# Beginning stage two with the token group that still lies in SBUF: order 2, 0, 1, 3

## The reference, cut to what matters

```
x = x + tanh(g_xattn) * (fake_quant(layernorm(x)) @ fake_quant(ctx))      # stage one
h = layernorm(x)                                                          # stage two
base = h @ base_W.T                                                       # 2048 x 2048
w = softmax top-2 of 8 experts, from h @ router_W.T
inc = ((h @ lora_A) * w) @ lora_B                                         # rank 16, 8 experts
x = x + tanh(g_ffn) * (base + 2.0 * inc)
```

## Time and profile before

| | us |
|---|---|
| median of three runs | 1121.61 |
| profiled execution, its time | 1117.15 |
| profiled execution, its span | 1115.4 |
| TensorE busy | 1027.0 (92%) |
| mean granted TensorE clock | 0.98 |

### The profile page before, as it was taken

The page is one execution under the profiler, slowest core; times in us unless marked ns, Lnnn a source line. Parts: engine busy times, 40 slices in busy tenths (PEclk is TensorE's granted clock), DMA queues, the critical chain, the costliest instruction groups (busy, mean ns, idle before and its releaser), DMA issues.

```text
span 1115.4 us, 12717 instructions
## 1 busy us (share of the span) xinstructions
PE 1027.0 (92%) x4827; PEld 762.8 (68%) x4848; DVE 768.4 (69%) x1046; ACT 448.1 (40%) x480; POOL 345.4 (31%) x181
## 2 busy tenths in 40 slices
PE   0588996999889999999999999899999989999998
PEld 0233442444378788788888878688887868888887
DVE  7696568882758754446778768986876898666554
ACT  5555155420043222223444445454444445434432
POOL 3685567769613433633100004400000350000000
PEclk9998998999979999999999999999999999999999
DMA  8998798887967787943585785568578456668754
GB/s 331 324 320 253 256 290 260 321 236 273 337 250 293 270 315 267 366 161 104 169 327 181 266 283 166 196 209 335 189 252 286 159 198 221 210 197 274 266 194 179
DMA packets 119052, 278.45 MB, mean 250 GB/s; under 512 B 40656, under 2 KB 48848, under 8 KB 110800
## 3 DMA queue, kind: packets, MB, share of 16 engines
q1 hardware_dynamic: 68048, 235.69, 59.1%
q10 hardware_dynamic: 50944, 41.95, 12.9%
HBM read 218.89 MB, written 50.33 MB: 241 GB/s over the span
## 4 chain that ended last, share of the span: by engine, by line
PE 68%; DVE 10%; DMA 7%; issue 4%; ACT 4%; POOL 4%; ACTq 2%; SPq 1%; POOLq 0%; DVEq 0%
PE acc L1380 16%; PE acc L1382 16%; PE acc L1381 16%; PE acc L1358 11%; DVE w_lo L1144 3%; DMA w_sums_scratch<-t_job 2%; DMA w_stage<-w_sums_scratch 2%; PE aT_psum L1450 2%; DMA out<-c_acc 2%; ACTq L808 2%; PE aT_psum L1428 1%; PE aT_psum L1429 1%; ACT ctx_u L795 1%; DVE A_lo L1245 1%; POOL ctx_quant L667 1%
## 5 line engine op out<-in xcount | busy, mean ns | idle before, releaser
L1144 DVE TENSOR_TENSOR w_lo<-w_stage,w_hi 128x1024 fp32r<-128x1024 f32 x200 | 268.0, 1351 | 170.1 <-ACT w_hi L853 169.2
L853 ACT ACTIVATE w_hi<-w_stage 128x1024 fp32r<-128x1024 f32 x200 | 209.6, 1058 | 355.5 <-PE acc L1382 266.0
L710 POOL TENSOR_TENSOR S_sum<-hT_A,hT_A 128x1024 f32<-128x1024 f32 x18 | 52.7, 2956 | 354.0 <-ACT hT_A L876 314.0
L1380 PE MATMUL acc<-w_hi,S_hi 128*128 128x512 f32 x384 | 152.2, 396 | 7.1 <-DVE w_lo L1142 5.9
L1358 PE MATMUL acc<-ctx_quant,aT_even 128*128 128x512 bf16 x503 | 118.2, 393 | 43.7 <-POOL ctx_quant L667 42.0
L1382 PE MATMUL acc<-w_hi,S_lo 128*128 128x512 f32 x384 | 150.7, 393 | 0.0
L1381 PE MATMUL acc<-w_lo,S_hi 128*128 128x512 f32 x384 | 150.4, 392 | 0.0
L1358 PEld LDWEIGHTS acc<-ctx_quant,aT_even 128*128 128x128 bf16 x512 | 50.9, 101 | 109.7 <-issue 45.4
L1358 PE MATMUL acc<-ctx_quant,aT_odd 128*128 128x512 bf16 x500 | 113.1, 384 | 6.8 <-POOL ctx_quant L667 5.8
L1380 PE MATMUL acc<-w_hi,A_hi 128*128 128x512 f32 x288 | 114.3, 397 | 3.5 <-DVE w_lo L1144 3.5
L1382 PE MATMUL acc<-w_hi,A_lo 128*128 128x512 f32 x288 | 112.4, 390 | 0.0
(11 more groups left out here) (174 smaller groups left out, 1672.5 us busy)
## 6 DMA issues: line engine op xcount, KB each, us to landing
w_stage<-in_wt SPq DMA_DIRECT2D x104, 512.0 KB, 4.4
w_stage<-w_sums_scratch SPq DMA_DIRECT2D x96, 512.0 KB, 4.3
ctx_stage<-in_ctx SPq DMA_DIRECT2D x32, 1024.0 KB, 7.6
t_job<-in_wt SPq DMA_DIRECT2D x8, 2048.0 KB, 9.6
w_sums_scratch<-t_job SPq DMA_DIRECT2D x8, 2048.0 KB, 14.3
c_acc<-x_scratch SPq DMA_DIRECT2D x32, 512.0 KB, 5.4
out<-c_acc ACTq DMA_DIRECT2D x64, 256.0 KB, 5.5
x_rows<-x_scratch SPq DMA_DIRECT2D x12, 1024.0 KB, 7.2
```

Source lines behind the costliest of these rows:

```text
L710: pool.tensor_tensor(half(dst, h), half(a, h), half(b, h), op).then_inc(combo_sum, 1)
L853: ins = act.activation(wh[i % HI][:, :], raw[:, :], ACT.Copy)
L1144: ins = dve.tensor_tensor(low[:, :], raw[:, :], high[:, :].bitcast(F32), ALU.subtract)
L1380: pe.matmul(out_, lh, rh, start=first, stop=False, skip_group_check=onto)
```

## The change

Stage two takes the groups in the order 2, 0, 1, 3 (`GROUPS`); rows for its loads and stores are computed with `GROUPS[g]` in place of `g`. Its first group is thus group 2, which at the end of stage one still lies in `xg[0]`. `load_group0` and its semaphores are gone. `group_stats` waits for `x1_ready` of the tile, and the first `normalise` (which writes in place) waits for group 2 to have been stored. B0 goes from 2440 to 2295, which moves the statistics to slots 2330 to 2435 and `normalise` to slots 2470 to 2575. The three early jobs get three places that don't overlap: job 2 no longer shares with job 0, and shares instead with job 1's neighbour in the `w_stage` ring. So job 2 is loaded at once behind job 1, all three jobs are stored in a row, the first AR pieces are loaded only after job 2 is stored, and `w_hi(0)` waits for job 0 alone. On POOL job 1 moves from slot 2260 to 2300 and job 2 from 2400 to 2420.

```diff
-B0 = 2440
+B0 = 2295
+GROUPS = (2, 0, 1, 3)
-JOB_A_SLOT = [2120, 2260, 2400]
+JOB_A_SLOT = [2120, 2300, 2420]
-        job_at = [CST, SMALL, CST, XG0, XG0 + 16 * KIB, XG1, XG0, XG0 + 16 * KIB]
+        job_at = [CST, SMALL + 4 * KIB, CST + 16 * KIB, XG0, XG0 + 16 * KIB, XG1, XG0, XG0 + 16 * KIB]
 def load_job(j):
                 if j == 2:
-                    sp.wait_ge(job_stored[0], 16)
+                    sp.wait_ge(c_conv, 2 * NB * CP)
 SP's queue:
             load_job(0)
             load_job(1)
+            load_job(2)
             store_job(0)
-            load_job(2)
-            sp.wait_ge(x1_stored[0], 16 * NB * 2)
-            load_group0()
             store_job(1)
-            sp.wait_ge(c_conv, 2 * NB * CP)
+            store_job(2)
             sp.wait_ge(job_stored[1], 16)
+            sp.wait_ge(job_stored[2], 16)
             for i in range(RAW - 1):
                 load_piece(i)
-            store_job(2)
             for a in range(2):
                 sp.wait_ge(x1_stored[a], 16 * NB * 2)
 ACT, w_hi:
                 elif i == 0:
-                    act.wait_ge(job_stored[2], 16)
+                    act.wait_ge(job_stored[0], 16)
 DVE:
             def group_stats(chain, g, m):
-                dve.wait_ge(g_in[m], 16)
+                dve.wait_ge(x1_ready, last_of_tile(M * GROUPS[0] + m) + 1)
             def normalise(chain, m):
+                if m == 0:
+                    dve.wait_ge(x1_stored[0], 16 * NB * 2)
```

More of the change, by code:

```diff
@@ L394, in build @@
         s_chain_b = sem("s_chain_b")
-        g_in = [sem(f"g_in{m}") for m in range(M)]
         xn_ready = sem("xn_ready")
@@ L513, in load_ctx @@
                     .then_inc(c_in[q % CS], 16)
-            def load_group0():
-                for m in range(M):
-                    sp.dma_start(xg[0][:, m, :], x1s[m * P:(m + 1) * P, :]).then_inc(g_in[m], 16)
             def load_piece(i):
@@ L567, in load_res @@
                     sp.wait_ge(out_stored[b], 32 * use)
-                r0, n = g * GT + (b if g == 0 else c_rows(g, s) // 2) * HT, c_col(g, s)
+                r0, n = GROUPS[g] * GT + (b if g == 0 else c_rows(g, s) // 2) * HT, c_col(g, s)
                 src = x1s[r0:r0 + HT, n * NW:(n + 1) * NW].rearrange("(t p) n -> p t n", p=P)
@@ L582, in load_row @@
                     sp.wait_ge(fill_done, 16 * (g - 1) + 12)
-                r0 = g * GT + m * P
+                r0 = GROUPS[g] * GT + m * P
                 sp.dma_start(row[m][:, :], x1s[r0:r0 + P, :]).then_inc(row_in[m], 16)
```

## The result

| | before | changed |
|---|---|---|
| median | 1124.71 us (15 runs) | 1119.21 us (15 runs) |
| first traced execution, its time | 1117.15 | 1127.19 |
| first traced execution, its span | 1115.4 | 1125.5 |

The ratio is 0.9948, 95% interval 0.9928 to 0.9969: 5.8 us faster (3.5 to 8.1), by 0.0052 x 1124.7. I had forecast 8.7 us and 1112.9, with 1108 to 1119 as the range. The measured time lies 0.2 us above it. (One run of 1325 us, at a granted clock of 0.757, is outside the ratio.)

What follows compares the result with a forecast made beforehand. TensorE, busy 1027 of 1115.4 us, was taken as the bound, so only idle and slow stretches could be won. 10.5 + 2.2 - 4.0 = 8.7 us gained, 1121.6 - 8.7 = 1112.9 us; range 1108 to 1119.

Steps and rivals of the forecast that it cites:

- the one behind step 6: After the AR product's step 6: TensorE's own pace and the same loads, all moved together, with no further gain or loss.
- the starting point of 1121.6: Median time taken for the kernel before, 4.5 us above the profiled execution's 1117.15.
- Gain at step 6: At the change of stage: the AR product's step 6 starts 8.7 us earlier than its 325.9.
- The new restart: After stage one's last unit: the AR product starts at 304.5 instead of 314.97, 10.5 us gained.
- The clock ahead of step 6: First six steps of the AR product: at full clock they take 8.7 us instead of 10.9, gaining 2.2 us.
- Piece 5: AR weight piece loaded after stage one's last store: it comes late, so TensorE idles 4.0 us before step 6 (2.8 to 7.2).
- The clock behind step 6: After the wait in front of the AR product's step 6: the forecast counted no loss from a fallen clock.
- the rival with the clock: TensorE's clock falls in the new wait before step 6, losing 2.0 to 2.2 us: gain 6.6, 1115.0; chance 0.26.
- Job 2 and the port: POOL beside DVE's four normalise: each costs job 2 0.97 us, so it ends at 291.9, ahead of stage one's end at 301.8.

Runs made afterwards that it cites:

- e3: The changed kernel with the jobs' old places and SP's old queue order put back; ratio to the kernel before 0.9930, median 1118.6 us.
- e6: The changed kernel with POOL's jobs 5 and 7 waiting until row tiles 1 and 3 are normalised; ratio to the kernel before 0.9882, median 1111.5 us.
- e9: The changed kernel with POOL's job 5 alone waiting until row tile 1 is normalised; ratio to the kernel before 0.9947, median 1119.9 us.
- e8: The kernel before with only POOL's jobs 5 and 7 put behind the row normalisations; ratio to the kernel before 0.9930, median 1118.3 us.
- e1: The changed kernel with AR piece 5 loaded ahead of the stored-x1 wait and residual loads; ratio to the kernel before 0.9920, median 1115.0 us.
- e5: e1 with the first three AR pieces split before the end of stage one; ratio to the kernel before 0.9915, median 1114.7 us.
- e7: e5 with AR pieces 6 and 7 also loaded ahead of the residuals, plus e6's edit; ratio to the kernel before 0.9820, median 1107.1 us.

## Why the prediction was off, by its own steps

The step that failed is the one behind step 6: "What follows is TensorE's own pace and the same loads, all moved together". Together with it, the starting point of 1121.6 was too low. Up to step 6 the forecast held.

- **Gain at step 6: 8.7 us. It held.** Step 6 came at 15.2, 15.0 and 16.2 us (15.4 forecast) for 24.1, 24.2 and 23.2 before: 8.4 us between the means. It is set by piece 5 alone, and each term of that chain was right within 0.2 us in the first trace. So the two terms ahead of the wait carry no weight in the sum as long as there is a wait: what the restart or the clock loses is taken off the wait.
- **The new restart: 10.5 us.** Measured 13.2 - 3.6 = 9.6. The missing 0.9 is the three `w_lo`, 2.20 for 1.14: I had priced POOL's contention for the `normalise` and job 2, but not for the instructions that set the restart. It made the wait for piece 5 shorter and cost nothing.
- **The clock ahead of step 6: 2.2 us.** This term was wrong in two of three traces: the clock fell behind the 2.3 us of idle time in front of the AR product, which I had put at 1.3 us and as harmless. It cost nothing either, for the same reason. And less was to be had than I thought: in the third trace of before the clock was full again at the AR product, and step 6 waited 1.3 us for piece 5 there as well.
- **Piece 5: -4.0 us.** It delayed step 6 by 2.9, 1.1 and 2.3 us, less than 4.0, mostly for what the restart and the clock had lost already.
- **The clock behind step 6: nothing counted. Here it failed.** From step 6 to the base it took 13.7 us in all traces of before, and in the two traces where the clock had fallen earlier. In the first trace, where it fell behind the wait for piece 5, it took 15.3, and so it did in e3 and e6 (15.1 in e9). So the rival with the clock was right in four of six traces, with 1.4 to 1.6 us for my 2.0 to 2.2. I had given it 0.26. I had cited the Trainium skill for it ("TensorE: Matmul & The Clock Gate", "HAM oscillation — how this bites in real kernels"), whose waits are of 3 to 5 us; the trace agrees as to the direction, and there 2.7 us were enough.
- **Job 2 and the port.** I had POOL lose 0.97 us in each of four steps. It lost 0.85 in one step; DVE paid instead, with `normalise` of 3.26 and 2.59 us for 1.34. That is nearer to the rule of the Trainium skill ("SBUF — State Buffer", "Who interferes with whom"), by which one side is blocked. Job 2 ended 13.3 us ahead of the end of stage one, for a forecast of 9.9. That its clock time was met within 1.3 us in the first trace is luck: stage one ended 2.1 us late there. It did not matter for the time.
- **Sum.** Of the 8.7 us, 8.4 are there at step 6 and 37.5 - 29.7 = 7.8 at the base in the three traces each (37.4 - 30.4 = 7.0 with e8 on the one side and e3, e6, e9 on the other). The runs say 5.8, with 7.0 and 7.8 inside the interval. The last 1 to 2 us I can't place: the rest differs by more than that between traces of one kernel (783.0 to 791.1). The clock fell once more near 385 us in all three traces of the changed kernel (0.89 in 376 to 392) and near 401 to 406 in two, and at neither place in the three of before (1.00). But TensorE waits 1.8 to 2.4 us near 385 in all six, e1, e5 and e9 have no such fall, and e8, from the kernel before, has one (0.95). Whether the change brings it is open.
- **The time itself: 1112.9 for 1119.2.** 3.1 us of this are the starting point: the three runs of before had a median of 1121.6, the fifteen have 1124.7. 3.2 are the gain, 5.5 between the medians for 8.7. The execution that I priced from (1117.15) was faster than any of the fifteen timed runs (lowest 1119.81), and its rest was 8 us shorter than in the two later traces; the 4.5 us that I added lifted it only to the median of three runs.

## What to carry to other kernels

When a chain of waits is cut at a change of stage, find the wait that ends last in the new chain: what is gained or lost ahead of it doesn't count, and what follows it (here a fallen clock) does. Price every instruction of the new chain with its new neighbours, above all the short ones on DVE beside POOL. Then look in the queues' order for the next transfer that is tied to an event which the change does not move. And compare stretches of several traces before trusting the span of one: here job 7 began 0.90 us behind the start of DVE's root (453.88) in the first trace and 0.19 us ahead of it (454.45) in the second, and that decided over a wait of 1.3 or 5.2 us and a fall of the clock.

## What the runs showed of the hardware

DVE operations on a single column took 2.17 to 2.20 us while a job step ran on POOL, and 0.16 to 0.22 with POOL waiting. A 128x2048 normalisation took 3.46 and 1.34. Statistics of 128x512 (L1014, four in 2.46 us) took the same beside job 1 as elsewhere. TensorE's clock went from 2.4 to 1.2 GHz behind idle times of 2.3 us (e1, its 0.87 and 0.70) and of 2.7 us (the changed kernel, 0.59), and in idle times of 5.2 us (0.77 over 15 us). It stayed at full in e5 and e7 with 0.6 us in front of the AR product. The length of the idle time alone doesn't tell: in front of the AR product it was 2.30 us in seven traces, behind the same work, and the clock fell there in three (the second and third of the changed kernel, e1) and not in four (the first, e3, e6, e9).
